# A Mamba2 mixer with two experts per token on one core: the next block's conv products placed ahead of the second couple's projection

## What is computed

```python
zxbcdt = x @ Win                                   # z, xBC, dt
xc = conv_b + sum(xp[:, k:k+l, :] * conv_w[k] for k in range(4))
xBC = silu(xc)                                     # xs, B, C
dt = softplus(dt + dt_bias); dA = exp(dt * -exp(A_log))
h = dA * h + (xs * dt) B ; y = h . C               # scan over the sequence
y = (y + D * xs) * silu(z)
x = x + rmsnorm(y, gnorm) @ Wout                   # x itself was rmsnormed first
```

## Time and profile before

| | |
|---|---|
| time, median of 3 runs | 1126.92 us (1123.45 to 1128.42) |
| the profiled execution: time, span | 1129.85 us, 1128.1 us |
| granted TensorE clock, mean | 0.971 |
| PE busy | 970.5 us, 86% of the span |
| DVE busy | 865.6 us, 77% |
| ACT busy | 768.0 us, 68% |
| POOL busy | 374.5 us, 33% |

### The profile page before, as it was taken

How to read it: one execution, slowest core, us unless ns; L and a number is a source line. 1 busy time by engine, 2 the same in 40 slices (tenths; PEclk the granted TensorE clock), 3 DMA queues, 4 the chain that set the end, 5 groups by cost and what they waited for, 6 DMA issues and landing times.

```text
span 1128.1 us, 47712 instructions
## 1 busy us (share of the span) xinstructions
PE 970.5 (86%) x20374; PEld 572.5 (51%) x20374; DVE 865.6 (77%) x1362; ACT 768.0 (68%) x1496; POOL 374.5 (33%) x415
## 2 busy tenths in 40 slices
PE   4789888989889888989988989888989987799877
PEld 2454544555445444445544545445454554458754
DVE  5689786988887897779888888797789875644356
ACT  3777777787678777777877778677877765123322
POOL 8512132141322311322323213232232223672555
PEclk9899999999999999999999999999999999699899
DMA  3403100100101101101010110011120010344631
GB/s 75 146 23 89 33 27 23 40 16 20 27 23 33 36 3 33 33 16 41 17 32 16 33 43 17 14 26 29 34 55 5 13 62 30 94 113 113 170 94 38
DMA packets 111722, 50.36 MB, mean 45 GB/s; under 512 B 85720, under 2 KB 104472, under 8 KB 111512
## 3 DMA queue, kind: packets, MB, share of 16 engines
q1 hardware_dynamic: 98040, 41.54, 14.1%
q0 software_dynamic: 3072, 3.15, 1.1%
q10 hardware_dynamic: 10400, 2.62, 1.0%
HBM read 24.66 MB, written 10.49 MB: 31 GB/s over the span
## 4 chain that ended last, share of the span: by engine, by line
PE 38%; issue 35%; POOL 10%; DVE 8%; ACT 5%; SPq 3%; DMA 0%; ACTq 0%; DVEq 0%; POOLq 0%
PE ring L1013 7%; POOL ysq L588 6%; PE ybank L1108 5%; PE ring L1047 4%; PE ring L1033 4%; PE oss L1120 3%; PE oss L1123 2%; PE ring L1065 2%; PE ring L1253 2%; DVE em L1886 2%; DVE yt L1893 1%; ACT xs L1468 1%; DVE yg L1906 1%; PE ybank L1269 1%; PE ring L965 1%
## 5 line engine op out<-in xcount | busy, mean ns | idle before, releaser
L1886 DVE TENSOR_TENSOR em<-em,gs 128x1536 f32<-128x1536 f32 (+1 forms) x192 | 300.7, 1585 | 11.2 <-ACT em L1449 10.7
L1449 ACT ACTIVATE em<-ring 128x512 f32<-128x512 f32 x480 | 248.8, 598 | 22.7 <-PE ring L1088 18.2
L1108 PE MATMUL ybank<-em,xdt 64*32 64x64 f32 (+1 forms) x12288 | 180.8, 237 | 28.7 <-issue 27.2
L588 POOL TENSOR_TENSOR ysq<-yg 128x512 f32<-128x512 f32 x96 | 110.7, 1153 | 279.2 <-DVE yg L1906 279.2
L1108 PEld LDWEIGHTS ybank<-em,xdt 64*32 64x32 f32 x12288 | 151.0, 105 | 90.7 <-issue 60.5
L1088 PE MATMUL ring<-rt,lt 128*64 128x512 bf16 x960 | 146.4, 393 | 17.7 <-ACT em L1449 11.4
L1914 DVE TENSOR_TENSOR on<-oss,rr 128x256 f32<-128x256 f32 x96 | 40.4, 421 | 79.9 <-ACT rr L1459 75.0
L1893 DVE SCALAR_TENSOR_TENSOR yt<-xs,col,ybank 128x256 f32<-128x256 f32 x192 | 83.0, 472 | 23.8 <-PE ybank L1108 23.8
L595 POOL TENSOR_TENSOR x_t<-on,x_b 128x256 f32<-128x256 f32 x48 | 41.8, 870 | 177.9 <-DVE on L1914 177.8
L595 POOL TENSOR_TENSOR x_b<-on,x_b 128x256 f32<-128x256 f32 x48 | 35.0, 730 | 195.4 <-DVE on L1914 195.4
L1088 PEld LDWEIGHTS ring<-rt,lt 128*64 128x64 bf16 x960 | 44.6, 109 | 103.2 <-issue 39.7
(11 more groups left out here) (286 smaller groups left out, 1829.9 us busy)
## 6 DMA issues: line engine op xcount, KB each, us to landing
rt<-wcat SPq DMA_DIRECT2D x80, 96.0 KB, 1.9
x_b<-x_t SPq DMA_DIRECT2D x48, 128.0 KB
cm<-bc SPq DMA_DIRECT2D x24, 224.0 KB, 2.6
rt<-lt SPq DMA_DIRECT2D x120, 24.0 KB
sorted_y<-yt ACTq DMA_DIRECT2D x10, 256.0 KB, 3.1
sorted_x<-h_b SPq DMA_DIRECT2D x4, 512.0 KB, 4.4
cw<-in_L_conv_t_cw SPq DMA_DIRECT2D x6, 320.0 KB
cw<-in_L_conv_b_cw SPq DMA_DIRECT2D x6, 320.0 KB
```

Source lines behind the costliest of these rows:

```text
L588: pool.tensor_tensor(out=ysq[c % 2][:], in0=yg[c % 2][:], in1=yg[c % 2][:], op=ALU.mult).then_inc(s_ysq, 1)
L1108: mm = pe.matmul(ybank[QUAD * q:QUAD * (q + 1), ab, to:to + hi - lo], xdt[m % 2][rows, 8 * (i % 2) + 4 * first + q, r, :], em[rows, p % EM ...
L1449: emptied(act.activation(em[:, p % EM_SLOTS, :, HALF * j:HALF * (j + 1)], o.rearrange("p (h t) -> p h t", h=HEADS), ACT.Exp), "seg", n, i, ...
L1886: dve.tensor_tensor(e, e, gs[n % 2][:, i:i + 1, 0:wide].to_broadcast([P, HEADS, wide]), ALU.mult).then_inc(s_w, 1)
```

## The change

On PE `project_x(n, 0)` stands in front of `project_out(k, 1)`; `project_out(k, 2)` stands behind `mix_states(k, 7)` and no longer behind z; `mean(n+1, 0)` stands behind the first two decays of block n, and the ring's list is changed with it. On ACT `inverse_root(k, 1)` stands behind the silus and their second table load, `inverse_root(k, 2)` behind the copies of the gram, `square_x(n+1, 0)` behind that, and `rstd_of(n+1, 0)` behind the first two exps of block n. On DVE `norm_out(k, 1)` stands behind `weigh(k, 7)`, `norm_out(k, 2)` behind `x_dt(n, 0)`, and `h_of(n, 0)` behind the first two weighs. POOL and SP keep their lists. No instruction is added or removed.

```diff
@@ ring_turns
         t.four("gram", n)
-        t.one("mean", n + 1, 0)
         t.seg(n, 0)
         t.seg(n, 1)
+        t.one("mean", n + 1, 0)
@@ PE
                 mix_states(k, 5)
+                if more:
+                    project_x(n, 0)
                 project_out(k, 1)
                 if more:
-                    project_x(n, 0)
                     turn_parts(n)
                     project_bc(n)
                     project_z(n, 0)
                     project_z(n, 1)
-                    project_out(k, 2)
                 mix_states(k, 6)
                 if more:
                     gram(n)
                 mix_states(k, 7)
-                if n + 1 < NBLOCK:
-                    mean(n + 1, 0)
+                project_out(k, 2)
                 if more:
                     turn_x(n, 0)
                     decays(n, 0)
                     decays(n, 1)
+                if n + 1 < NBLOCK:
+                    mean(n + 1, 0)
@@ ACT
                     scale_x(n)
-                inverse_root(k, 1)
                 if more:
                     act.preload_act_table_set("silu_and_others")
                     silu_x(n, 0)
                     silu_tapped(n)
                     silu_bc(n)
-                if n + 1 < NBLOCK:
-                    square_x(n + 1, 0)
-                if more:
                     silu_z(n, 0)
                     silu_z(n, 1)
                     act.preload_act_table_set("natural_log_exp_and_others")
                 if k % 2 == 0 and k >= 2 and pass_of(k) + 1 < NPASS:
                     exp_a(pass_of(k) + 1)
-                inverse_root(k, 2)
+                inverse_root(k, 1)
                 if more:
                     copy_gram(n)
+                inverse_root(k, 2)
                 if n + 1 < NBLOCK:
-                    rstd_of(n + 1, 0)
+                    square_x(n + 1, 0)
                 if more:
                     exps(n, 0)
                     exps(n, 1)
+                if n + 1 < NBLOCK:
+                    rstd_of(n + 1, 0)
@@ DVE
-                if k and more:
+                weigh(k, 0)
+                weigh(k, 1)
+                if more:
                     h_of(n, 0)
-                weigh(k, 0)
-                if k == 0:
-                    h_of(1, 0)
-                weigh(k, 1)
...
                     rows_of_cum(n)
-                norm_out(k, 1)
                 x_dt(k, 3)
                 weigh(k, 6)
                 weigh(k, 7)
-                if more:
-                    norm_out(k, 2)
+                norm_out(k, 1)
                 add_skip(k, 3)
                 gate_y(k, 3)
                 if more:
                     x_dt(n, 0)
+                norm_out(k, 2)
```

## The result

| | before | after |
|---|---|---|
| median | 1126.53 us (4 runs) | 1147.01 us (4 runs, 1142.78 to 1151.15) |
| profiled execution: time, span | 1129.85, 1128.1 us | 1142.78, 1141.0 us |
| granted TensorE clock, mean | 0.971 | 0.961 |

The ratio is 1.0184 (95% interval 1.0140 to 1.0229): slower by 1.8%, outside the range of the forecast.

A forecast was written before the change was run, and what follows sets the result against it. No engine is full; each turn is a DVE-bound interior plus a tail where PE and ACT alternate. Gains of 5.9 and 8.1 less losses of 3.2, 0 and 2.0 make 8.8 us: median 1118, own range 1111 to 1124.

The forecast's parts named there:

- the row of POOL times in the turns with weights: POOL, ten even turns: weights end near 583.0, then add_x(k,2) 0.85 and square_y(k,3) 1.04 to 1.4 us.
- Rival 2: POOL becomes the bound: each POOL step at the interior's start takes a weigh of 1.2 us more; 1135.5 us, chance 0.12.
- (a): Order alone, 13 turns without weights: 0.45 us gained in each, 5.9 us in all.
- (b): PE stalls in the tails of the 13 turns without weights become covered, at most 0.9 each: 8.1 us gained.
- (e): PE's 1.02 us wait for POOL no longer covers four stops inside mix_states(k,5): 2.0 us lost.
- The order on ACT: ACT in the tail of turn 13: exps(n,0) 2.5 us earlier, exps(n,2) 1.15 us earlier.
- the 1.5 for `weigh(n,2)`: DVE, turn 13: the second couple's first weigh starts at 585.95 instead of 587.49, 1.5 us earlier.
- rival 1: PE's stops are moved, not covered: 1126 us with half the cover, 1134 with none; chance 0.25.
- (c): Five weight turns, band kind: 8.75 us lost, 5.5 of stalls covered under that wait, so 3.2 lost.
- (d): Five weight turns, time kind: 2.25 us lost, 2.3 of stalls covered, so nothing.
- The signs: If right: DVE's norm_out wait about 1.7 us, ACT's sums wait gone, PE's square wait moved, odd turns 1 to 1.5 shorter.

The follow-up runs named there:

- run 5: Changed kernel with one operand of each block's first two weighs read from PSUM, mix_states(n,0) waiting for both; timing only: 1127.4 us, 0.9997 to the kernel before.
- its control: The kernel before with the same PSUM operand for the first two weighs and the same mix_states wait: 1132.5 us, ratio 1.0035 to the unedited kernel before.
- run 3: Changed kernel with POOL's weights moved ahead of add_x(k,1) and square_y(k,3) ahead of add_x(k,2): 1121.77 us, ratio 0.9914 to the kernel before.
- run 7: Changed kernel with project_out(k,3) on PE moved behind turn_x(n,1) and decays(n,2): 1146.08 us, ratio 1.0152 to the kernel before.
- run 1: Changed kernel with only POOL's weights moved ahead of add_x(k,1): 1132.87 us, ratio 1.0022 to the kernel before.

## Why the prediction was wrong

**The step that failed** is the row of POOL times in the turns with weights: "add_x(k,2) 0.85, square_y(k,3) 1.04 to 1.4", and with it the reading of the earlier trace rows, that neighbours cost about 0.5 us. The 2.19 of the earlier trace rows and the 1.67 of the earlier trace rows, taken as "beside a weigh" and "elsewhere", were both locked. In turn 10 L522 takes 0.68, and the trace of the kernel before had that length too, where no DVE instruction stood beside it:

```profile
44.37 0.68 POOL L522 TENSOR_TENSOR win<-win,col 128x296 f32<-128x296 f32 x1
```

The difference of two locked times is no price. The price is the rest of the other engine's instruction: 0.9 to 1.0 on `add_x(k,2)`, in turns 2, 6 and 10, and 1.0 to 1.5 on the square, in eight turns.

**Rival 2 is what happened**, with a chance of 0.12 and a price of 1135.5. Its mechanism and its sign were right. The rule behind it (the Trainium skill, SBUF — State Buffer, "SBUF: two separate sides") agrees with turn 10's 1.76 and 2.02, and run 5 shows the other side of it, 1.04 once the weigh has one operand from SBUF. Its size was too small: one weigh of 1.2 was charged in each of the ten turns with weights. Seven of these and turn 22, which has none, were held, three of them in both POOL steps, and each lost 1.9 to 3.7 us. It had 17.4 us off the forecast; the changed kernel, at 1.0184, lies 2.2% or 25 us above run 5 set against its control (0.9962). How much of the 21.9 us that the eight turns lost is the half clock was not separated; run 3, which is fast with eight such stretches, and run 7 speak against its being the larger part.

**Terms (a), (b) and (e)** came to 12.0 together. The eleven odd turns got 8.94 us shorter, k = 0 1.34, but turn 22 2.91 longer: 7.4. The order on ACT came nearly as worked out (turn 13 above). Most of what is missing on DVE is the weigh held by the square, 0.8 of 1.0 us in turn 13, which the 1.5 for `weigh(n,2)` did not have. The rest belongs to rival 1: the cover in (b) was taken near its upper bound, and stops still delayed ACT. In the loop it waited 6.7 us for PE in front of `root(k,2)`, nearly all in turns with such a stop (0.84 in turn 13), and 11.3 us in run 3.

**Terms (c) and (d)**: 3.2 and 0 lost, measured 13.0 and 6.6. The weights were taken as 4.8 us; in turn 10 they take 3.3 (466.37 to 469.63) where no weigh stands beside them. So even the reason why POOL was to be late was too dear by 1.5, and the loss was larger all the same. In (d) turns 4 and 20, whose squares were locked, lost 6.1 of the 6.6.

**The signs.** DVE's wait before `norm_out(k,1)` is 2.3 us per turn, where 1.7 was forecast and 3.1 stood before `norm_out(k,2)`. PE's wait for POOL moved to `project_out(k,3)`, as the text said; it is 1.4 to 3.6 us in the eight long turns, where the text had 1 to 3. ACT's wait for the sums did not vanish (30.0 for 42.5): it moved to `root(k,2)` and `root(k,3)`, 6.7 and 20.2 of it. Odd turns gained 0.81, not 1 to 1.5; even band turns lost 2.6.

**What held.** With the square out of the lock (run 3) the change is worth 0.9% (interval 0.5 to 1.2), where 8.8 us or 0.8% was forecast. That the two nearly agree is in part luck: run 3 moves the weights out of the way, so its 7.6 us stand against the 12.0 without (c). Open: why PE stops where the trace shows no releaser; no run here touched that.

## What to carry to other kernels

When a reorder changes the time at which a POOL step runs, look at which DVE instruction now stands beside it: if both read SBUF and DVE's has two operands there, price the later one at the whole rest of the earlier one, and take a step's own length from a place where neither neighbours it. Put the POOL step that others wait for first in its list, so that it runs while DVE waits, and move slack work such as weights to where nobody needs the step behind it. A mean duration that grows while the instructions stay the same is the first sign.

## What was not expected of the hardware

- A lead of some hundredths of a us decides the lock: 0.08 ahead gave 1.04 for the square (turn 13), 0.04 behind gave 2.08 (run 1, turn 6).
- The same instruction has two lengths by its neighbour alone: L522 0.68 in turn 10, 1.67 and 2.19 in the earlier trace rows; L524 0.19 in turn 10, and a mean of 1.14 before.
- Reading one operand from PSUM freed POOL's step altogether: 0.97 us behind the weigh's start, and 1.04 long.
- A PE that stood still for 3.6 us came back at a granted clock of 0.50, and kept it for 3.4 us.
